# Two relation layers of a graph network: fixed chunk ranges in place of loops over computed bounds, and a tile's next-table products inside the next tile's visits

## What is computed

```python
def _rgcn_layer(x, W, b, src, dst, edge_type, num_nodes):      # W: 8 x 256 x 256
    xt = jnp.einsum('ni,rio->rno', x, W)
    msg = jax.nn.relu(xt[edge_type, src] + b)
    return jax.ops.segment_sum(msg, dst, num_segments=num_nodes)

h = jnp.maximum(_layernorm(x, axis=-1), 0.0)
h = _rgcn_layer(h, W0, b0, ...)
h = _rgcn_layer(h, W1, b1, ...)
return x + h
```

## Time and profile before

| | us |
|---|---|
| three timed runs | 3314.57, 3300.53, 3320.32 (median 3314.57) |
| the profiled execution | 3310.53 |
| its span, first to last instruction | 3308.7 |
| first gather of `rel1` | 1841.0 |
| first gather of `rel2` | 2643.44 |

### The profile page before, as it was taken

The page is one execution under the profiler, slowest core; times in us unless marked ns, Lnnn a source line. Parts: engine busy times, 40 slices in busy tenths (PEclk is TensorE's granted clock), DMA queues, the critical chain, the costliest instruction groups (busy, mean ns, idle before and its releaser), DMA issues.

```text
span 3308.7 us, 38710 instructions
## 1 busy us (share of the span) xinstructions
PE 2512.1 (76%) x12405; PEld 1894.0 (57%) x12406; DVE 1308.5 (40%) x2954; ACT 556.4 (17%) x1692; POOL 818.3 (25%) x867
## 2 busy tenths in 40 slices
PE   6699999997998999999999475575464734554455
PEld 4588888886554788877767243343342423433344
DVE  7778888874666211133233122222222311222122
ACT  1255555553000000011112100010010100000000
POOL 2000000000000000000000565454545166566664
PEclk9799999998999999999999677787787867767677
DMA  2022222222553444444443433333333333333332
GB/s 66 16 105 90 101 96 90 90 105 87 194 190 117 159 150 151 148 137 134 141 153 100 138 108 96 99 119 93 101 98 97 100 90 93 86 87 87 89 98 66
DMA packets 144187, 361.12 MB, mean 109 GB/s; under 512 B 21408, under 2 KB 85006, under 8 KB 144042
## 3 DMA queue, kind: packets, MB, share of 16 engines
q1 hardware_dynamic: 45940, 194.06, 16.9%
q0 software_dynamic: 39936, 109.11, 11.6%
q10 hardware_dynamic: 58166, 56.07, 4.9%
HBM read 242.08 MB, written 117.07 MB: 109 GB/s over the span
## 4 chain that ended last, share of the span: by engine, by line
PE 60%; issue 15%; DVE 11%; another core or an unknown queue 8%; ACT 2%; DVEq 2%; DMA 1%; PEld 0%; PEldq 0%; ACTq 0%; SPq 0%; POOL 0%; POOLq 0%
PE agg L929 20%; PE agg L980 12%; PE y L749 11%; PE agg L829 5%; PE y L790 3%; PE prod L742 3%; DVE gathered L1417 1%; PE turn_ps L727 1%; ACT gathered L1088 1%; PE agg L818 1%; PE y L793 1%; DVE y_sb L1384 1%; DVE onehot L1696 1%; DVE slot_hot L1394 1%
## 5 line engine op out<-in xcount | busy, mean ns | idle before, releaser
L655 POOL DMA_INDIRECT gathered<-table_rel,idx_rel x832 | 799.1, 960 | 2449.9 <-DMA table_rel<-t_sb 1863.1
L980 PE MATMUL agg<-gathered,onehot 128*128 x2048 | 568.2, 441 | 391.3 <-issue 303.3
L980 PEld LDWEIGHTS agg<-gathered,onehot 128*128 128x128 f32 x2048 | 447.2, 223 | 518.9 <-issue 448.1
L1696 DVE SCALAR_TENSOR_TENSOR onehot<-iota,tilebase,edges 128x256 f32<-128x256 f32 x512 | 242.8, 485 | 1094.8 <-PE agg L980 484.8
L929 PE MATMUL agg<-t_sb,stream 128*128 128x256 f32 (+1 forms) x1875 | 379.3, 364 | 8.4 <-DMA stream<-counts_dense 8.4
L929 PE MATMUL agg<-gathered,stream 128*128 128x256 f32 (+1 forms) x1875 | 379.4, 361 | 0.0
L929 PEld LDWEIGHTS agg<-t_sb,stream 128*128 128x128 f32 (+1 forms) x1875 | 300.3, 160 | 83.3 <-issue 11.4
L929 PEld LDWEIGHTS agg<-gathered,stream 128*128 128x128 f32 (+1 forms) x1875 | 298.6, 159 | 73.1
L829 PE MATMUL agg<-h_sb,stream 128*128 128x257 f32 x1250 | 336.7, 394 | 0.0
L1029 ACT COPY turned<-turn_ps 128x256 f32<-128x256 f32 (+2 forms) x100 | 40.3, 403 | 1443.2 <-PE turn_ps L727 1161.3
L749 PE MATMUL y<-relw,turned 128*128 128x512 f32 x400 | 227.4, 732 | 48.0 <-issue 31.2
(11 more groups left out here) (186 smaller groups left out, 1966.7 us busy)
## 6 DMA issues: line engine op xcount, KB each, us to landing
table_rel<-y_sb ACTq DMA_DIRECT2D x176, 256.0 KB
stream<-weights_dense SPq DMA_DIRECT2D x50, 832.0 KB, 4.4
stream<-counts_dense SPq DMA_DIRECT2D x50, 800.0 KB, 4.3
stream<-weights_dense SPq DMA_DIRECT2D x50, 768.0 KB, 4.3
weights_dense<-stream SPq DMA_DIRECT2D x25, 832.0 KB, 3.4
weights_dense<-stream SPq DMA_DIRECT2D x25, 768.0 KB, 3.2
gathered<-table_rel,idx_rel POOLq DMA_INDIRECT x832
counts_dense<-t_sb SPq DMA_DIRECT2D x25, 416.0 KB, 4.0
```

What stands on the lines that cost most here:

```text
L655: pool.indirect_dma_start(gathered[:, slot * D:(slot + 1) * D], None, tables[n], bass.IndirectOffsetOnAxis(ap=idx_rel[:, c:c + 1], axis=0) ...
L980: mm = pe.matmul(agg[b][:, 0:width], onehot[:, half_ * QUAD + k, :], gathered[:, bass.ds((q & (GQ - 1)) * (QUAD * D) + k * D, width)], sta ...
L1696: nc.vector.scalar_tensor_tensor(onehot[:, at:at + 2, :], iota[:].unsqueeze(1).broadcast_to([P, 2, P]), tilebase[:, bass.ds(t, 1)], pair[: ...
```

## The change

In the regular case both layers are written out without loops or registers, over `window(t)`; the old code stays for the irregular case, behind an `If` on each of PE, DVE, ACT and SP. SP no longer passes on landings; PE waits on `s_scat` itself. PE turns and multiplies tile t-1 at the middle chunk of tile t's range, DVE copies its sum there too, and DVE's bias additions for t-1 follow behind its one-hots of tile t. The gathers (L648 to L658) stay as they are.

```diff
+    PAIRS = [(window(t)[1] - window(t)[0]) // 2 for t in range(TILES)]
+    def middle(t):
+        return window(t)[0] + PAIRS[t] // 2 * 2
+    def last_tile(quad):
+        return max(t for t in range(TILES) if window(t)[0] < (quad + 1) * QUAD and window(t)[1] > quad * QUAD)
...
@@ SP
-            for pi, n in enumerate(RELS):
-                if n == "rel1":
-                    for g in range(REL // 2):
-                        sp.wait_ge(pair_stored[g], 16 * TILES + 1)
-                    load_relations(rel_w1, rel_b1, s_wrel[1])
-                for q in range(QUADS):
-                    sp.wait_ge(s_scat[q % GQ], (q // GQ + pi * ROUNDS + 1) * (16 * QUAD))
-                    sp.sem_inc(quad_landed, 1)
+            for g in range(REL // 2):
+                sp.wait_ge(pair_stored[g], 16 * TILES + 1)
+            load_relations(rel_w1, rel_b1, s_wrel[1])
+            with sp.If(irregular(sp) > 0):
...
@@ PE
+            def tile_visits(n):
+                before = RELS.index(n)
+                def visits(t):
+                    lo, hi = window(t)
+                    pe.wait_ge(agg_free, before * TILES + t + 1)
+                    for c in range(lo, hi):
+                        if c == middle(t) and n == "rel1" and t >= 1:
+                            for _, part in parts[n]:
+                                part(t - 1, (t - 1) % 2)
+                        quad, pair = c // QUAD, before * sum(PAIRS) + sum(PAIRS[:t]) + (c - lo) // 2
+                        if c == lo or c % QUAD == 0:
+                            pe.wait_ge(s_scat[quad % GQ], (quad // GQ + before * ROUNDS + 1) * (16 * QUAD))
+                        if c % 2 == 0:
+                            pe.wait_ge(onehot_ready, pair + 1)
+                        slot = c % GRING
+                        mm = pe.matmul(agg[t % 2][:, 0:D], onehot[:, pair % QUAD * 2 + c % 2, :],
+                                       gathered[:, slot * D:(slot + 1) * D], start=c == lo, stop=c == hi - 1)
+                        if c % 2:
+                            mm.then_inc(pair_free, 1)
+                        elif c % QUAD == 0 and c > lo and last_tile(quad - 1) == t:
+                            mm.then_inc(quad_free, 1)
+                    pe.drain().then_inc(agg_ready, 1)
+                return visits
...
-                over_tiles(pe, visits_of(n), parts[n])
+            with pe.If(irregular(pe) > 0):
+                for n in RELS:
+                    over_tiles(pe, visits_of(n), parts[n])
+            with pe.Else():
+                for n in RELS:
+                    for t in range(TILES):
+                        tile_visits(n)(t)
+                    for _, part in parts[n]:
+                        part(TILES - 1, (TILES - 1) % 2)
...
@@ ACT
-            over_tiles(act, None, parts["rel1"])
-            with act.Fori(0, TILES - 1) as t:
+            with act.If(irregular(act) > 0):
+                over_tiles(act, None, parts["rel1"])
+            with act.Else():
+                for t in range(TILES):
+                    copy_turned("rel1", KB, t)
+                    finish_relations("rel1", "rel2", t)
+            for t in range(TILES - 1):
...
@@ DVE
-            over_tiles(dve, visits_of("rel1"), [(1, rel1_rows), (2, lambda t, b: relations("rel1", t))])
-            over_tiles(dve, visits_of("rel2"), [(1, rel2_rows)])
+            def tile_onehots(n):
+                before = RELS.index(n)
+                def visits(t):
+                    lo, hi = window(t)
+                    for c in range(lo, hi, 2):
+                        if c == middle(t) and n == "rel1" and t >= 1:
+                            rel1_rows(t - 1, (t - 1) % 2)
+                        pair = before * sum(PAIRS) + sum(PAIRS[:t]) + (c - lo) // 2
+                        dve.wait_ge(pair_free, pair + 1)
+                        at = pair % QUAD * 2
+                        nc.vector.scalar_tensor_tensor(onehot[:, at:at + 2, :],
+                                                       iota[:].unsqueeze(1).broadcast_to([P, 2, P]),
+                                                       tilebase[:, t:t + 1],
+                                                       edges[:, c:c + 2, 1:2].broadcast_to([P, 2, P]), ALU.add, ALU.is_equal
+                                                       ).then_inc(onehot_ready, 1)
+                return visits
...
+                for t in range(TILES):
+                    tile_onehots("rel1")(t)
+                    if t >= 1:
+                        relations("rel1", t - 1)
+                rel1_rows(TILES - 1, (TILES - 1) % 2)
+                relations("rel1", TILES - 1)
+                static_tiles(tile_onehots("rel2"), after["rel2"])
```

More of the change, by code:

```diff
@@ L565, in _ @@
                     load_relations(rel_w0, rel_b0, s_wrel[0])
-            for pi, n in enumerate(RELS):
-                if n == "rel1":
-                    for g in range(REL // 2):
-                        sp.wait_ge(pair_stored[g], 16 * TILES + 1)
-                    load_relations(rel_w1, rel_b1, s_wrel[1])
-                for q in range(QUADS):
-                    sp.wait_ge(s_scat[q % GQ], (q // GQ + pi * ROUNDS + 1) * (16 * QUAD))
-                    sp.sem_inc(quad_landed, 1)
+            for g in range(REL // 2):
+                sp.wait_ge(pair_stored[g], 16 * TILES + 1)
+            load_relations(rel_w1, rel_b1, s_wrel[1])
+            with sp.If(irregular(sp) > 0):
+                for pi, n in enumerate(RELS):
+                    for q in range(QUADS):
+                        sp.wait_ge(s_scat[q % GQ], (q // GQ + pi * ROUNDS + 1) * (16 * QUAD))
+                        sp.sem_inc(quad_landed, 1)
             sp.wait_ge(s_out, 16 * TILES)
@@ L997, in _ @@
             pe.sem_inc(quad_free, GQ)
[L998 to L1002, removed]
-                over_tiles(pe, visits_of(n), parts[n])
+            pe.sem_inc(S["rel1", "y_added"], REL // 2)
+            pe.wait_ge(s_wrel[1], 16 * (KB + 2))
+            pe.sem_inc(S["rel1", "rows_turned"], 1)
+            with pe.If(irregular(pe) > 0):
[7 more added lines that the diff above has]
+                        part(TILES - 1, (TILES - 1) % 2)
         @block.scalar
@@ L1178, in _ @@
                                   (1, "root"), (1, "copy_normed"), (2, "finish"), (1, "finish"))))
-            over_tiles(act, None, parts["rel1"])
-            with act.Fori(0, TILES - 1) as t:
+            with act.If(irregular(act) > 0):
[5 more added lines that the diff above has]
+            for t in range(TILES - 1):
                 act.wait_ge(S["rel2", "table_ready"], t + 1)
-                act.dma_start(out[bass.ds(t * P, P), :], xt(t)).then_inc(s_out, 16)
+                act.dma_start(out[t * P:(t + 1) * P, :], xt(t)).then_inc(s_out, 16)
             act.wait_ge(S["rel2", "table_ready"], TILES)
@@ L1717, in _ @@
             dve.wait_ge(s_wrel[1], 16 * (KB + 2))
-            over_tiles(dve, visits_of("rel1"), [(1, rel1_rows), (2, lambda t, b: relations("rel1", t))])
-            over_tiles(dve, visits_of("rel2"), [(1, rel2_rows)])
+            def tile_onehots(n):
[14 more added lines that the diff above has]
+                return visits
+            after = {"rel1": [(1, rel1_rows), (2, lambda t, b: relations("rel1", t))], "rel2": [(1, rel2_rows)]}
+            with dve.If(irregular(dve) > 0):
+                for n in RELS:
+                    over_tiles(dve, visits_of(n), after[n])
+            with dve.Else():
+                for t in range(TILES):
[5 more added lines that the diff above has]
+                static_tiles(tile_onehots("rel2"), after["rel2"])
 _INS = ["x", "src", "dst", "edge_type_8", "edge_weight", "L0_gnn_w_self", "L0_gnn_w_neigh", "L1_gnn_W1",
```

## The result

The changed kernel takes 3163.81 us (median of 4 runs, 3152.92 to 3169.0), the kernel before, on the same chip, 3312.99 (4 runs): a ratio of 0.9549, 95% interval 0.951 to 0.9588. It is 4.5% faster, where 11% were forecast; 3164 lies outside the range (2915 to 3115). The profiled run took 3165.84 us, with a span of 3164.0.

The account below looks back on a forecast made before the run. PE's stop at each tile's end was taken as the bound, filling the 32-chunk ring. 1841 + 525 + 26 + 525 + 12 + 15 = 2944 us span, 2946 with 1.8 around, 2950 as median; range 2915 to 3010, to 3115 with B and C.

Parts of the forecast that it names:

- The gather is next: Relation layers: with PE's and DVE's stops gone, POOL's gathers are last, 525 us a layer from first to last gather.
- 525 + 26 + 525 + 12: Forecast times of `rel1`'s gathers, the pause between the layers, `rel2`'s gathers and the end after the last gather, in us.
- the 15 us put down for PE's excess and the `If`s: 10 us for PE exceeding POOL's pace in `rel1`, 5 us for the flag loads and taken branches at 1857.
- the drains, forecast near 1 us: PE's drain at each tile's end: its record, 9.2 us in the middle before, would be near 1 us.
- Loops, bounds, register waits go: Relation layers, on PE, DVE, ACT: PE's "issue" idle (292.9 us in `rel2`) and DVE's "remote" idle go nearly whole.
- the pitch: POOL's gather-to-gather time, 1.252 us, taken from 48 gathers started without waiting; 520 us for a layer's 416.
- D: Relation layers: PE's stop is drain and signals during gathers and stays; 106 us of added visits, 3395 us; chance 0.07.
- 360 us: Whole kernel: the forecast gain between the time now and the forecast, 7 us for each of the 50 tiles.
- Rival E: Tile ends: half the stops stay, as branches were only half of the stop; 3130 us; chance 0.08.
- B: Relation layers: POOL's "remote" waits of 3.2 us come with the gathers, one a tile; 154 more, 3104 us; chance 0.13.
- C: `rel1`: PE is the bound at a clock of 0.76, 94 us in place of 10; 3034 us; chance 0.12.
- as the forecast had weighed it: One-hots beside gathers: the skill's rule would cost 145 us a layer, about 3240; the trace did not agree.

Follow-up runs that it names:

- e9: The changed kernel unedited, in a group without late signals: 2936.24 us against 2937.7 for the kernel before, ratio 0.9999.
- e18: The kernel before, unedited, in profile, in a group where signals are prompt: 2935.19 us.
- after: The changed kernel's first profiled run, with late signals: 3165.84 us, span 3164.0.
- e15: The changed kernel with a ring of 16 pairs of one-hots and no drain, with late signals: 3099.61 us, 0.9406 of the kernel before.
- e10: The changed kernel with products behind the tile again, loops still written out, with prompt signals: 2975.51 us, 1.0131 of the kernel before.
- e11: The changed kernel with exact ranges, 464 chunk visits a layer in place of 600, with prompt signals: 2934.48 us, 0.9986 of the kernel before.
- e3: The changed kernel with one column of a pair's one-hots written in place of 128, from the fifth pair on: 3176.9 us, one run.
- e5: The changed kernel unedited, in a group with late signals: 3171.87 us, 0.9649 of the kernel before (3291 us).
- e6: The changed kernel with POOL waiting after every eighth gather until it has landed: 3131.66 us, 0.9544 of the kernel before.
- e7: The changed kernel with POOL filling an unused buffer and waiting for the fill after every fourth gather: 3132.28 us, 0.9529 of the kernel before.
- e4: The changed kernel with POOL's gathers replaced by as many SP loads of the same size, rows in order: 2615.23 us, one run.
- e12: The changed kernel with gathers of 64 rows in place of 128 from the 33rd on, with prompt signals: 2899.52 us, one run.

## Why the prediction was wrong

**The bound.** "The gather is next" is right, and so is its price. Where signals are prompt (e9) the changed kernel takes, by my terms, 530 + 24.5 + 529 + 10.8 us for 525 + 26 + 525 + 12, and 2936 in all for 2950; the 15 us put down for PE's excess and the `If`s do not show. PE in `rel1` is 85% busy (450.18 of 529.9) at a clock of 0.96, as forecast; the drains, forecast near 1 us, take 2.1.

**The step that failed** is the first of the sum: "Loops, bounds, register waits go ... PE's idle by issue and DVE's remote idle should go nearly whole." I read the stop between PE's last matmul and DVE's next one-hot as the drain, the loop's end and the loads of the bounds. e18 has all three and no such stop; after has none but the drain, and 217.6 us of idle by issue in `rel2`. The stops are lateness: in these groups, once POOL has run over 8 gathers on end, PE's and DVE's steps wait microseconds for what has long happened. That signals are late the trace's own record of `pair_free` shows; that PE's own steps can be too, e15. What makes them late, and why only in some groups, stays open. The earlier trace rows held it in plain sight: 48 gathers on end, PE and DVE still. I noted it, and used it only for the pitch and for D.

**The gain.** I forecast 360 us. With prompt signals the change is worth 0, since the kernel before is at POOL's pace too. There the two differ by terms that cancel: pause 34.0 to 24.5 and end 12.9 to 10.8 are won; `rel1` +4.0, `rel2` +4.9 and the start +2.9 are lost. The two layers' 8.9 are the longer gathers, 808.2 for 799.0 us, beside 88 more one-hots. With late signals it is worth 119 to 149 us in the three groups that have both kernels (3313 to 3164, 3291 to 3172, 3296 to 3167).

**Rival E** (3130: branches were half of the stop) came nearest in time, by luck: with prompt signals the branches cost nothing. **B** (POOL keeps stopping, 3104) was next, and its sign is there: POOL's "remote" waits in `rel2` stayed at 41.5 us, 14 times. But they don't come with the gathers as such, for with prompt signals there are none (e9), and they were never one a tile: 13 in 25 tiles of `rel2` and 2 in `rel1` before. **C** (PE bound in `rel1`) did not happen where signals are prompt: POOL has no wait over 0.3 us for PE (e9); e10 shows how near it is. **D** named the place, signals of PE while gathers run, and missed the sign: I added 106 us for visits that are hidden (e11: 2 us for 136 fewer a layer, with prompt signals), and took a stop's length as fixed, where it fell by half in `rel1`. That fewer steps of an engine's own code mean fewer late ones (38710 instructions before, 34009 after) is my reading of the gain with late signals; it is argued, not shown.

**One-hots against gathers.** With one-hots cut to a column (e3) the stops stayed, and a gather took 945 ns for 969: 24 ns x 832 / 600 = 0.033 us for each one-hot. The rule of the Trainium skill ("SBUF — State Buffer", "Who interferes with whom"), that the ports which DVE and GpSimd share are an exclusive lock, would, taken for these two instructions, make it 0.484 us each; these runs show an effect of its sign and a fifteenth of that size, as the forecast had weighed it.

## What to carry to other kernels

When two engines stand still in the same stretch, look at what a third is doing before putting it down to their own code, and sort the lateness of a signal by how long that third engine has been at it. A pitch found in a stretch where the others stood still is a floor and not a forecast. Put the kernel under study, unedited, into each group of runs: here the kernel before moved by 375 us between groups, more than any edit that kept the gathers, and a change can be worth 4.5% in one group and nothing in the next.

## What the runs showed of the hardware

- In four of the six groups a one-hot starts 0.04 us (median) after it could while POOL has run fewer than 8 gathers on end, 1.7 us after at 8 to 11, 4.5 at 16 to 23, up to 10.7 beyond 24 (after, e5). A pause of POOL of some 2 us resets it (e6); a fill of 0.54 us after every fourth gather keeps it at 0.32 (e7).
- It is there in some groups of runs and absent in others, on the same chip and for the same kernel, with gathers, landings and dense stages alike.
- Loads of the same size issued by SP, of rows in order, don't bring it (e4).
- With 16 pairs of one-hots and no drain PE also stops between the two records of one product, 39 times over 1 us (e15), where it waits for no signal.
- A gather of 64 rows took 893 ns at best and 903 in the middle (e12), one of 128 rows 941 at best and 947 in the middle: halving the rows saved 5%.
- A drain's record was 1.7 us in the middle and 4.5 at most with prompt signals, 9.2 and 33 with late ones, for the same code (e18 and before); for the changed kernel 2.1 and 5.4 (e9) against 3.8 and 23 (after). Here its length tells more of late signals than of PE's work.
